# Normalization with a masked batch norm: TensorE's program as a loop over five units, and the stores of the last six whole tiles behind the last loads in the sync queue

## The reference

```python
def _gn(v, G=32, eps=1e-5):           # group norm: 2 channels per group
    g = v.reshape(B_, G, C_ // G, H_, W_)
    m = jnp.mean(g, axis=(2, 3, 4), keepdims=True)
    s = jnp.var(g, axis=(2, 3, 4), keepdims=True)
    return ((g - m) / jnp.sqrt(s + eps)).reshape(v.shape)

def _L0_conv_ref(x):                  # batch norm over the places whose channel sum isn't 0
    x1 = x.sum(axis=1)
    m = x1 != 0
    ...                               # counts, padding to the largest count, mean and variance per channel
    inv = 1.0 / jnp.sqrt(var + EPS)
    out = jnp.where(m[:, None, :, :], x * inv[None, :, None, None], x)
    ...
```

## Time and profile before

| | us |
|---|---|
| three executions | 1277.38, 1277.55, 1278.63 |
| median | 1277.55 |
| the profiled execution, its own time | 1278.15 |
| its span in the trace | 1276.4 |
| TensorE, VectorE, ScalarE, GpSimd busy | 743.7, 764.6, 816.3, 495.1 |
| mean rate of the 16 DMA engines over the span | 421 GB/s |

### The profile page before, as it was taken

The page is one execution under the profiler, slowest core; times in us unless marked ns, Lnnn a source line. Parts: engine busy times, 40 slices in busy tenths (PEclk is TensorE's granted clock), DMA queues, the critical chain, the costliest instruction groups (busy, mean ns, idle before and its releaser), DMA issues.

```text
span 1276.4 us, 10694 instructions
## 1 busy us (share of the span) xinstructions
PE 743.7 (58%) x2882; PEld 303.7 (24%) x2882; DVE 764.6 (60%) x1894; ACT 816.3 (64%) x950; POOL 495.1 (39%) x504
## 2 busy tenths in 40 slices
PE   0777654576545675456765556654577545675436
PEld 0222221222212222222222222222122212222212
DVE  7766556565565566655665556556565665566634
ACT  0877555775556765567755578555776556775555
POOL 0055333453334443334433345333453334443330
PEclk9988767887768877678876788777887767877678
DMA  9999999999999999999999999999999999999976
GB/s 397 416 430 429 430 430 429 431 430 431 429 431 429 431 429 431 429 432 428 431 429 432 430 431 428 433 428 427 431 423 429 420 428 428 422 428 428 424 329 264
DMA packets 39084, 537.58 MB, mean 421 GB/s; under 512 B 4336, under 2 KB 4336, under 8 KB 6896
## 3 DMA queue, kind: packets, MB, share of 16 engines
q1 hardware_dynamic: 21168, 276.83, 51.2%
q10 hardware_dynamic: 17856, 260.05, 47.7%
HBM read 268.44 MB, written 268.44 MB: 421 GB/s over the span
## 4 chain that ended last, share of the span: by engine, by line
DMA 61%; ACT 17%; PE 10%; DVE 6%; issue 5%; SPq 0%; ACTq 0%; DVEq 0%
DMA out_dram<-slots 37%; DMA slots<-in_x_dram 24%; ACT slots L377 11%; PE flush L454 6%; ACT fresh L373 5%; DVE stats L508 2%; PE small_ps L417 1%; PE stay L450 1%; PE stay L451 1%; PE small_ps L427 1%; DVE spread L487 1%; PE small_ps L428 1%; ACT sums L373 0%; DVE dev L554 0%; DVE spread L528 0%
## 5 line engine op out<-in xcount | busy, mean ns | idle before, releaser
L508 DVE BATCH_NORM_STATS2 stats<-slots 128x6 f32<-128x512 f32 x1024 | 632.4, 681 | 458.0 <-DMA slots<-in_x_dram 456.5
L377 ACT ACTIVATE slots<-slots,out_bias,out_scale 128x1024 f32<-128x1024 f32 x512 | 623.1, 1247 | 2.0 <-DVE out_bias L565 1.2
L355 POOL TENSOR_TENSOR sums<-fresh,sums 128x512 f32<-128x512 f32 x360 | 459.2, 1275 | 374.9 <-ACT fresh L373 374.9
L454 PE MATMUL flush<-slots,weights 128*64 128x512 f32 x1536 | 443.6, 698 | 40.9 <-ACT fresh L373 39.3
L373 ACT ACTIVATE fresh<-flush,group_bias 128x512 f32<-128x512 f32 x360 | 247.7, 688 | 51.8 <-PE flush L454 51.8
L454 PEld LDWEIGHTS flush<-slots,weights 128*64 128x64 f32 x1536 | 132.1, 156 | 294.3 <-issue 293.5
L389 ACT ACTIVATE by_image<-by_image,eps 128x4 f32<-128x4 f32 x32 | 9.5, 297 | 262.6 <-DVE by_image L532 262.0
L333 POOL TENSOR_TENSOR weights<-pair_sum,group_rstd 128x64 f32<-128x64 f32 x128 | 33.7, 294 | 361.0 <-DVE group_bias L545 361.0
L417 PE MATMUL small_ps<-stats,group_avg 128*128 128x64 f32 x64 | 21.5, 436 | 207.1 <-DVEq L521 207.1
L450 PE MATMUL stay<-slots,weights 128*64 128x512 f32 x512 | 139.7, 605 | 0.0
L451 PE MATMUL stay<-minus_mean,weights 128*64 128x512 f32 x512 | 138.1, 593 | 0.0
(11 more groups left out here) (54 smaller groups left out, 203.5 us busy)
## 6 DMA issues: line engine op xcount, KB each, us to landing
slots<-in_x_dram SPq DMA_DIRECT2D x127, 2048.0 KB, 18.5
out_dram<-slots ACTq DMA_DIRECT2D x124, 2048.0 KB, 28.9
out_dram<-slots SPq DMA_DIRECT2D x16, 512.0 KB, 5.5
slots<-in_x_dram SPq DMA_DIRECT2D x4, 512.0 KB, 23.5
```

The source lines that it names most:

```text
L355: pool.tensor_tensor(into, fresh[:, n % FRESH_BUFS, :], into, ALU.add).then_inc(added, 1)
L377: nc.scalar.activation(out_in_ring(u, i), image_in_ring(u, i), ACT.Identity, bias=out_bias[:, u % 2, t:t + 1], scale=out_scale[:, u % 2, t ...
L454: nc.tensor.matmul(into, weight, source, start=True, stop=True).then_inc(image_summed, 1)
L508: last = V.bn_stats(stats[:, u % 2, k * BLOCK_STATS:(k + 1) * BLOCK_STATS], source)
```

## The change

There are two parts. TensorE's program is no longer written out: unit 0 stands by itself, then a loop of six turns, each with five units (1 to 30), then unit 31 by itself. The numbers that the waits compare with are computed in the loop from the turn. For addresses to repeat from turn to turn, the buffers taken by `u % 2` are now three, taken by `buf(u)`, and the last unit's negative weights have a tensor of their own. The second part: the six stores of tiles 118 to 123 (the last two tiles of unit 29, the four of unit 30) are no longer issued by ScalarE but by SyncE, behind the last loads and ahead of the last unit's 16 stores.

```diff
+BUFS = 3
+TURN = 5
...
+    def buf(u):
+        return BUFS - 1 if u in (0, LAST) else (0, 1, 2, 0, 1)[(u - 1) % TURN]
...
-        weights = sb("weights", [P, 2, 2, SETS, ROWS])
+        weights = sb("weights", [P, BUFS, SETS, ROWS])
+        last_weights = sb("last_weights", [P, SETS, ROWS])
...
-        stats = sb("stats", [P, 2, UNIT_BLOCKS * BLOCK_STATS])
+        stats = sb("stats", [P, BUFS, UNIT_BLOCKS * BLOCK_STATS])
...
+            for j in range(TILES - RING, TILES - UNIT_TILES):
+                sp.wait_ge(out_ready, (j + 1) * TILE_CHUNKS)
+                sp.dma_start(in_dram(out_rows, j), tile_in_ring(j)).then_inc(stored[j % RING], 16)
             for i in range(B):
                 sp.wait_ge(out_ready, LAST * B + i + 1)
                 sp.dma_start(chunk_in_dram(out_rows, LAST, i), out_in_ring(LAST, i)).then_inc(last_stored, 16)
...
             def store(u, t):
                 j = u * UNIT_TILES + t
-                act.wait_ge(out_ready, (j + 1) * TILE_CHUNKS)
-                act.dma_start(in_dram(out_rows, j), tile_in_ring(j)).then_inc(stored[j % RING], 16)
+                if j < TILES - RING:
+                    act.wait_ge(out_ready, (j + 1) * TILE_CHUNKS)
+                    act.dma_start(in_dram(out_rows, j), tile_in_ring(j)).then_inc(stored[j % RING], 16)
...
-            def statistics(u):
-                small(u * SMALLS + 1, mean_ps, group_avg[:, :], triples(u)[:, :, :, 1])
+            def statistics(u, ago):
+                smalls = ago * (TURN * SMALLS) + u * SMALLS
+                small(smalls + 1, mean_ps, group_avg[:, :], triples(u)[:, :, :, 1])
...
-                        pe.wait_ge(weights_ready, u * SETS + set_order(u).index(t) + 1)
+                        pe.wait_ge(weights_ready, ago * (TURN * SETS) + u * SETS + set_order(u).index(t) + 1)
...
-                            wait_for_bank(pe, before, flush_order(before)[(m - FLUSH_BANKS) % ADDS])
+                            earlier = flush_order(before)[(m - FLUSH_BANKS) % ADDS]
+                            if u < LAST:
+                                pe.wait_ge(taken, ago * (TURN * ADDS) + taken_with(before, earlier))
+                            else:
+                                wait_for_bank(pe, before, earlier)
...
-            for u in range(UNITS):
-                statistics(u)
-                channel_sums(u)
+            statistics(0, 0)
+            channel_sums(0, 0)
+            with pe.Fori(0, (UNITS - 2) // TURN) as turn:
+                for u in range(1, 1 + TURN):
+                    statistics(u, turn)
+                    channel_sums(u, turn)
+            statistics(LAST, 0)
+            channel_sums(LAST, 0)
```

More of the change, by code:

```diff
@@ L80, in norm_conv_kernel @@
                         for t in (x, out))
+    assert TURN * UNIT_TILES % RING == 0 and TURN * len(flushed) % FLUSH_BANKS == 0 and (UNITS - 2) % TURN == 0
+    def buf(u):
+        return BUFS - 1 if u in (0, LAST) else (0, 1, 2, 0, 1)[(u - 1) % TURN]
     def set_of(i):
@@ L129, in norm_conv_kernel @@
         pair_sum = sb("pair_sum", [P, ROWS])
-        minus_mean = sb("minus_mean", [P, 2, SETS])
+        minus_mean = sb("minus_mean", [P, BUFS, SETS])
         minus_pair_sum = sb("minus_pair_sum", [P, ROWS])
@@ L443, in channel_sums @@
                             before = (m - FLUSH_BANKS) // ADDS
-                            wait_for_bank(pe, before, flush_order(before)[(m - FLUSH_BANKS) % ADDS])
+                            earlier = flush_order(before)[(m - FLUSH_BANKS) % ADDS]
[3 more added lines that the diff above has]
+                                wait_for_bank(pe, before, earlier)
                     for k in range(BLOCKS):
                         into = bank[k * ROWS:(k + 1) * ROWS, :]
-                        weight = weights[:, u % 2, 1 if u == LAST and i in flushed else 0, t, :]
+                        weight = last_weights[:, t, :] if u == LAST and i in flushed else weights[:, buf(u), t, :]
                         source = image_in_ring(u, i)[:, k * BLK:(k + 1) * BLK]
@@ L450, in channel_sums @@
                             nc.tensor.matmul(into, weight, source, start=u == 0, stop=False)
-                            nc.tensor.matmul(into, weight, minus_mean[:, u % 2, t:t + 1].to_broadcast([P, BLK]),
+                            nc.tensor.matmul(into, weight, minus_mean[:, buf(u), t:t + 1].to_broadcast([P, BLK]),
                                              start=False, stop=u == LAST).then_inc(image_summed, 1)
@@ L507, in block_stats @@
                 source = in_ring(j).rearrange("p i n -> p (i n)")[:, k % TILE_BLOCKS * BLK:(k % TILE_BLOCKS + 1) * BLK]
-                last = V.bn_stats(stats[:, u % 2, k * BLOCK_STATS:(k + 1) * BLOCK_STATS], source)
+                last = V.bn_stats(stats[:, buf(u), k * BLOCK_STATS:(k + 1) * BLOCK_STATS], source)
                 if k == UNIT_BLOCKS - 1:
@@ L515, in statistics @@
                 at = slice(u * SETS, (u + 1) * SETS)
-                mean, rstd, bias = group_mean[:, at], group_rstd[:, at], group_bias[:, u % 2, :]
+                mean, rstd, bias = group_mean[:, at], group_rstd[:, at], group_bias[:, buf(u), :]
                 means, squares = triples(u)[:, :, :, 1], triples(u)[:, :, :, 2]
@@ L524, in statistics @@
                 link(V.tensor_reduce(mean, mean_ps.rearrange("p (i f) -> p i f", f=FOLDS), AX_X, ALU.add))
-                note(V.tensor_scalar(minus_mean[:, u % 2, :], mean, -1.0, None, ALU.mult))
+                note(V.tensor_scalar(minus_mean[:, buf(u), :], mean, -1.0, None, ALU.mult))
                 link(V.tensor_tensor(dev[:, :, :], means, over_folds(mean), ALU.subtract))
@@ L589, in count @@
                     dve.wait_ge(added, taken_with(LAST - 2, i))
-                    V.scalar_tensor_tensor(out=not_zero[:, i, :], in0=bank_of(LAST, i), scalar=group_bias[:, LAST % 2, set_of(i):set_of(i) + 1],
+                    V.scalar_tensor_tensor(out=not_zero[:, i, :], in0=bank_of(LAST, i), scalar=group_bias[:, buf(LAST), set_of(i):set_of(i) + 1],
                                            in1=sums[:, flushed.index(i), :], op0=ALU.subtract, op1=ALU.not_equal,
```

37 lines of the change are left out of this document (18 added, 19 removed).

## The result

The changed kernel takes 1269.15 us in the median (1268.86 to 1269.76, 4 runs), the kernel before 1277.8 beside it (4 runs): a ratio of 0.9931, 95% interval 0.9919 to 0.9944. That is 8.65 us less, and the forecast of 1269.7 is 0.55 off. The profiled execution took 1269.24, its span is 1267.5.

A forecast was written before the change was run, and what follows sets the result against it. The kernel was taken to be bound by its DMA transfers, with a hole at the end. Moving the stores wins 7.8 us, the loop 0: 1278.15 - 7.8 = 1270.3 profiled, 0.6 less for the median, 1269.7; range 1264.5 to 1273.

The forecast's parts named there:

- (a): Trailing engines until store 117 has landed, at 1207.26: nothing changes.
- (b): Trailing engines after 1207.26: same tiles in another order, without a gap, ending at 1245.6 again; tile 127 lands at 1217.
- (c): Last unit starts earlier: ScalarE decides, root at 1230.7, 14.5 us earlier; first output by 1237.2, last at 1254.2.
- (d): Last 16 stores begin at 1245.6, where store 123 ends, without a hole; 20.8 to 22.1 us, 22.1 taken.
- (e): End of the span: 1245.6 + 22.1 + 0.9 = 1268.6, 7.8 us less than 1276.4.
- The engines ahead: Fourteen DMA engines get a new gap before the last load, finish at 1243.5 and don't bind, by only 2 us.
- Its cover: TensorE's lateness per unit hidden in steady state: 10.5 us of waits plus 13 us of queued stores, 23 us.
- (1): Rival: the loop removes TensorE's code fetches from the trailing engines, up to 8 us more won, 1262 to 1266; chance 0.12.
- (2): Rival at the end: only 0 to 5 us won, 1272.5 to 1277, by late fourteen engines or slow SyncE; chance 0.08.
- (3): Rival: TensorE's loop code is fetched in each turn as before, 1269.7 to 1271, inside the forecast; no separate chance.
- (4): Rival: the branch back stops TensorE longer than the 23 us hidden; a 27 us stop gives 1290; chance 0.04.

The follow-up runs named there:

- The run with the whole load: Kernel before with tile 127 loaded whole instead of in four pieces, stores left where they were: 1268.19 us (0.9926).
- with ten: Changed kernel with three loop turns of ten units in place of six of five: 1269.76 us (0.9936).
- the combination with the whole load: Changed kernel with tile 127 loaded whole instead of in four pieces: 1270.81 us (0.9952).
- The run without a dip: Changed kernel with only unit 30's four stores moved, 118 and 119 back on ScalarE: 1268.77 us (0.9929).
- the doses: Changed kernel with 90 or 160 matmuls that nobody reads at the start of each turn: 1326.94 us (1.0386) and 1509.39 us (1.1815).

## Why the prediction was right

**The view that carried it.** The DMA share of 0.10 to 0.13 in the earlier trace rows was read as two engines of 16. The packet records bear it out: from 1237.5 to 1245.3 there are two chains of packets and no more. From that came the price: not the 15.7 us that the mean engine stood still, but what those two stood still. The gain was 8.65.

**Steps (a) and (b)**, that the trailing engines have the same work up to store 123, in another order: 1245.6 was expected, 1246.4 measured. The pieces of tile 127 landed 7.5 us after their issue, by 1217 as expected.

**Step (c)**, that ScalarE decides: the root at 1230.47 (1230.7 expected), the first output begun at 1235.76 and the last done at 1253.98 (1254.2). TensorE was free at 1224.98 (1225.1), so the numbers computed in the loop don't delay it at unit 30. VectorE was through at 1220.3, where 1221.4 was expected; half of that was a slip, since the ten blocks of the earlier trace rows end at 1204.97 + 6.09 = 1211.1 and not at 1211.6. It lies off the path.

**Step (d)** is the term that was mis-sized. I took 22.1 us for the 16 last stores, from the stage of the kernel before, out of concern for code fetches; it took 1266.7 - 1246.4 = 20.3, 1.27 each, just under the other end (20.8). From 1245.6 to 1254 the rate was 417 GB/s, above the 404 of the kernel before in that stage. With (b) 0.8 too short, (d) 1.8 too long and 0.1 in (e), the span came out at 1267.5 where 1268.6 was forecast. That the time in the median is off by 0.55 and not by this 1.1 is luck: the forecast took off 0.6 because the profiled execution before lay that much above its median, and the profiled one of the changed kernel lies 0.1 above its own.

**The engines ahead** were expected to get a gap that doesn't bind. They got it (0.80 and 0.54), and with the run with four stores moved no cost of it shows. That they don't bind by some 2 us is about right too: at store 123 the last engine lands 2.8 us behind the fourteenth, by the landing records.

**Part two** was taken at 0, and the loop alone gives 0.9998. Its cover was put at 23 us; for one stop in a turn it is 30. The rival of a slower kernel needed a stop over that, so its point lay further off than I wrote.

**The cause**, on the other hand, I had only half. The sum 1.3 + 4.88 = 6.2 for the distance of the pieces stands in the prediction, and with it the reason, a small piece for a whole tile of stores; but I took from it that the six stores hold up the load, whatever its packets. The run with the whole load shows that they could have stayed: 1268.19 without moving one. The forecast came right all the same, since moving the stores removes the turns too.

The rivals: (1) the loop relieves the trailing engines, refuted by the loop alone; (2) less is won, not seen; (3) code fetched anew, not the case with five units, and of no cost that shows with ten; (4) slower by the branch back, not seen.

## What to carry to other kernels

Where two queues share the DMA engines, compare their packet sizes before anything else: a load in 4 KB packets beside stores in 16 KB ones got a fifth of an engine here, and splitting a critical transfer "to get its first part sooner" can make its last part the latest of all. Price a hole in the DMA share by the engines that end last, not by the mean. Ask also which engines are late: a DMA has landed when the last of its engines has, and here two of sixteen decided. And a code loop on an engine that waits a good part of each round cost nothing that shows, whether or not its code stayed on chip; a stop had to be longer than 30 us to be seen.

## What was not expected of the hardware

- Two of the 16 DMA engines trail the others, in the kernel before by 8 us after 1237 us (a share of 0.10 to 0.13 until 1245.6). The trace's records don't number the engines, so which two they are isn't known. They fall behind bit by bit over the whole run: by the landing records of the stores, the last engine is 0.7 us behind the fourteenth at 58 us, 6.4 at 469, and 12.1 at 1207, the other 9.8 there. 19 packets of TensorE's code less didn't change the end, and more code on ScalarE barely did.
- After the dip the engines count as busy and move less: between 1209 and 1217 a share of 1.01 at 380 GB/s in the changed kernel. Single packets take longer between 1207 and 1216: those of 4 KB 0.20 us in the mean instead of 0.16, and in the combination with the whole load those of 16 KB up to 1.15 in the mean of a microsecond instead of 0.61. The run without a dip is at 424 GB/s:

```profile
1209.00:1217.00 8.00, 8.00 (x40) 3.54 (x39) 3.05 (x6) 8.00 (x10) 5.15 (x5) 1.00 1.02 424
```

- TensorE's small dummy matmuls went at 0.22 us an instruction, two to a call in f32, 256 columns each. By the earlier trace rows a call of 512 columns is two instructions as well (512 for four kept images, two blocks and 32 units, which are 256 calls), which I had overlooked when I sized the doses.
- A branch back to code that has to be fetched again, with 27 packets on q8 over the whole run, did not lengthen TensorE's wait at unit 11 (5.78 us) beyond that at other units.
